# Two attention layers on one Trainium2 core: the second softmax by rows, its halves turned by DMA, outputs tile by tile

## The chip, the cores and the metric

The kernel runs on 1 core of one Trainium2 chip. The metric is the device time of one execution in microseconds (us). The engines are TensorE (PE, with its weight loads PEld), VectorE (DVE), ScalarE (ACT), GpSimd (POOL) and the sequencer that issues most DMAs, SyncE (SP).

## The reference

Input x has 8 images of 32 x 32 tokens and 256 channels. Two residual blocks follow one another; each begins with a group norm without weights.

```python
# block A: 32 windows (rows of the image), 8 heads of 32 channels
qkv = einsum('bnwc,cd->bnwd', gn(x), w_qkv)
attn = softmax(einsum('bhnqd,bhnkd->bhnqk', q, k) * 32 ** -0.5)
x = x + einsum('bnwc,cd->bnwd', attn_times_v, w_proj) + b_proj
# block B: all 1024 tokens, one head, q and k of 32 channels, v of 256
energy = einsum('bid,bjd->bij', k, q)
x = x + gamma * einsum('bij,bjc->bic', softmax(energy), v)
```

## The kernel before

One image after the other passes through both blocks, and three images are in work at once: in step `i` block B of image `i`, block A's attention of image `i+1` and the norm and q, k, v of image `i+2`. Each engine's program is written out by hand in this order: a function `first(i, ...)` and a function `second(i, ...)` per engine, called by `all_steps` (line 229), with a hardware loop over the steps 2 to 4. Engines run in order and meet in semaphores.

All products that need float32 accuracy are made of three f16 products, `split3` (lines 250 to 252): high by high, high by low, low by high. A tensor therefore exists as a high half and a low half (the rest).

**Block A** of an image: `transposes`, statistics and norm (`a_nh`, `a_nl`), q/k projection (`a_project_qk`, 48 products of 512 columns into `pa`), V projection (`a_project_v`, 48 of 256), `a_scores` (line 461, after `k_spread` has laid k out as a block diagonal by 8 DMAs), softmax in windows of 32 (`a_maximum`, `a_exponential`, `a_row_sum`, `a_probabilities` on POOL, `a_transpose`), `p_spread` (8 DMAs, line 340), `a_output` (line 484), the output's high parts on ACT (`a_out_high`, line 718) and low parts on DVE (`a_out_low`, line 875), `a_regroup` (16 DMAs, line 318), `a_projection` (48 products of 256 columns) and the residual (`a_residual`, line 884).

**Block B**: `transposes` of x1, norm, `b_project_qk`, `b_project_v`, `b_stacks` (4 DMAs, lines 304 to 307, which lay high and low of q and k above one another). Then the energies are made twice. `b_energy` (line 536) makes them by rows, only for the maximum of each row, `b_maximum` (line 904). The maxima are put as two more rows into `k_stack` (`b_max_rows`, line 543), and `b_energy_T` (line 554) makes the energies again, transposed and with the maximum taken off. ACT makes the exponential, which is then already in the layout that the output product needs: `e_h` (line 743) on ACT for five of the eight tiles and as a cast on DVE for three, `e32` (line 744), and the rest `e_l` on DVE (line 919). `b_output` multiplies all eight tiles of `e` with V; a 257th column of ones in V gives the row sum. `b_result` on DVE divides and adds.

In step `i` the `first` half of PE holds the outputs of image `i-1` with the energies of image `i` between them, the `second` half the transposed energies of image `i` with the projections of the other two images between them. So block B of one image stretches over two steps.

Of the kernel before, what the change touches and what calls it, by code (L numbers as in the profile page):

```python
# [35 lines left out]
P = 128  # L36
# [9 lines left out]
DVE_HIGH = (1, 3, 4)  # L46
VCOL = CH + 2
EPS = 1e-5
ROW_SCALE = 2.0 ** 15
# [6 lines left out]
def build(nc, x, w_qkv, w_proj, b_proj, wq1, wk1, wv1, gamma, ident_d, group_d, masks_d, out):  # L56
# [3 lines left out]
    with ExitStack() as ctx:  # L60
# [3 lines left out]
        def sem(name):  # L64
            return ctx.enter_context(nc.semaphore(name))

# [23 lines left out]
        xb = sb("xb", [P, TILES, CH])  # L90
        x1 = sb("x1", [P, TILES, CH])
# [17 lines left out]
        y = sb("y", [P, TILES, CH])  # L109
# [4 lines left out]
        q_stack = sb("q_stack", [P, TOKENS], F16)  # L114
        k_stack = sb("k_stack", [P, TOKENS], F16)
        v_h, v_l = sb("v_h", [P, TILES, VCOL], F16), sb("v_l", [P, TILES, VCOL], F16)
        max_neg = sb("max_neg", [P, TILES])
        max_hl = sb("max_hl", [P, TILES, 2], F16)
        ident_h = sb("ident_h", [P, P], F16)
        e32 = sb("e32", [P, 2, TOKENS])  # L120
        e_h, e_l = sb("e_h", [P, TILES, TOKENS], F16), sb("e_l", [P, TILES, TOKENS], F16)
        y_inv = sb("y_inv", [P, TILES])
        y_fac = sb("y_fac", [P, TILES])

# [5 lines left out]
        stage = e_l[:].rearrange("p t n -> p (t n)").bitcast(F32)  # L130
# [15 lines left out]
        s_ident = sem("s_ident")  # L146
# [10 lines left out]
        a_load = [sem(f"a_load{c}") for c in range(CHUNKS)]  # L157
        a_xb = sem("a_xb")
# [22 lines left out]
        b_copy = sem("b_copy")  # L181
# [9 lines left out]
        b_mxh = sem("b_mxh")  # L191
        b_mxl = sem("b_mxl")
        b_row = sem("b_row")
        b_rows = sem("b_rows")
        b_st = sem("b_st")
        b_exp = sem("b_exp")
        b_eh = sem("b_eh")
        b_el = sem("b_el")
        b_pv = sem("b_pv")
        b_yinv = sem("b_yinv")  # L200
        b_yfac = sem("b_yfac")
        b_y = sem("b_y")
# [20 lines left out]
        bufs = {"a": dict(src=xin, xT=a_xT, nh=a_nh, nl=a_nl, ps=pa, col=384, mean=3, var=2, **norm["a"], **{"s_" + k: v for k, v in n_["a"].items()}),  # L223
                "b": dict(src=x1, xT=b_xT, nh=b_nh, nl=b_nl, ps=pb, col=0, mean=2, var=3, **norm["b"], **{"s_" + k: v for k, v in n_["b"].items()})}

        def after(eng, s, value):

            if not (isinstance(value, int) and value <= 0):
                eng.wait_ge(s, value)

        def all_steps(eng, first, second):

            def peeled(half, i):
                half(i, *(0 <= n < IMAGES for n in (i, i - 1, i + 1, i + 2)))

            for i in range(-1, 2):
                peeled(first, i)
                peeled(second, i)
# [44 lines left out]
        def _(sp):  # L283
# [58 lines left out]
            def first(i, b, o, m, f):  # L342
                if m: p_spread(i + 1, 0)
# [782 lines left out]
```

## Time and profile before

| | us |
|---|---|
| median of 3 runs | 705.11 (704.42 to 709.46) |
| the profiled execution, its own time | 708.19 |
| its span, first to last instruction | 706.1 |
| PE busy in the span | 600.7 (85%) |
| DVE busy | 493.9 (70%) |
| ACT busy | 321.7 (46%) |
| POOL busy | 152.0 (22%) |

The rows come from the profiled execution; its own time is 2.1 us above its span. An engine's busy time counts its computing instructions alone. A PE product is shown longer than its share of the engine, since products are pipelined; the steps of the chain of work show the time between two of them. The granted clock is the share of TensorE's full clock. A DMA is issued by a sequencer (SPq is SP's), and "to landing" counts from the issue to the semaphore.

### The profile page before, as it was taken

To read this page: it belongs to the slowest core of one execution; us is meant where nothing else is said; L and a number is where in the kernel's file an instruction comes from. 1 tells how busy PE (TensorE), PEld (TensorE's weight loads), DVE (VectorE), ACT (ScalarE), POOL (GpSimd) and SP (SyncE) were. 2 spreads that over 40 slices of the span, in tenths; PEclk is the share of its full clock that TensorE was granted. 3 is DMA by queue.
4 is the path that set the end of the run, shared out by engine and by line. 5 is a ranking of instruction groups with operands and counts; after the bars stand their busy time and mean duration, and the time that the engine had idled before them with its cause. 6 is when DMAs were issued, how large, how long until landed. Compare 5 with 4: busy or idle time off the path is not lost. (4 is left out here: it accounts for less than half of the span.)

```text
span 706.1 us, 14862 instructions
## 1 busy us (share of the span) xinstructions
PE 600.7 (85%) x5859; PEld 433.6 (61%) x5859; DVE 493.9 (70%) x829; ACT 321.7 (46%) x422; POOL 152.0 (22%) x130
## 2 busy tenths in 40 slices
PE   2475794799998999899998999899989989649987
PEld 2255472547785677657774778567765767336756
DVE  4445267667976888577976797597967796775654
ACT  2423443476228741675228632774157611750261
POOL 5502232213114202303213311411230321000000
PEclk9996896789999999999999999999999999878999
DMA  4042313231241225031323223122504103201101
GB/s 156 0 121 61 90 32 94 50 82 38 84 105 51 61 54 145 33 88 31 104 82 82 51 82 104 48 56 48 145 26 105 31 24 106 76 0 38 43 4 60
DMA packets 40306, 47.51 MB, mean 67 GB/s; under 512 B 6848, under 2 KB 32320, under 8 KB 40256
## 3 DMA queue, kind: packets, MB, share of 16 engines
q1 hardware_dynamic: 36960, 43.47, 23.5%
q10 hardware_dynamic: 3296, 3.34, 1.4%
q8 instruction: 35, 0.57, 0.4%
q14 instruction: 15, 0.12, 0.1%
HBM read 10.09 MB, written 8.39 MB: 26 GB/s over the span
## 5 line engine op out<-in xcount | busy, mean ns | idle before, releaser
L250 PE MATMUL pb<-v_h,e_h 128*128 128x257 f16 x464 | 127.6, 275 | 1.7 <-DVE y L929 1.6
L252 PE MATMUL pb<-v_h,e_l 128*128 128x257 f16 x464 | 126.5, 273 | 0.0
L251 PE MATMUL pb<-v_l,e_h 128*128 128x257 f16 x464 | 126.1, 272 | 0.0
L904 DVE TENSOR_REDUCE max_neg<-pb 128x1 f32<-128x1024 f32 x64 | 77.5, 1210 | 42.6 <-PE pb L536 42.2
L919 DVE TENSOR_TENSOR e_l<-e,e_h 128x1024 f16<-128x1024 f32 x64 | 77.8, 1223 | 18.9 <-ACT e L744 17.3
L744 ACT ACTIVATE e<-pb,f_energy 128x1024 f32<-128x1024 f32 x64 | 71.3, 1114 | 23.1 <-PE pb L554 23.1
L554 PE MATMUL pb<-k_stack,q_stack 98*128 98x512 f16 x128 | 39.3, 389 | 29.8 <-ACT k_stack L735 19.9
L718 ACT ACTIVATE before_turn<-pa 128x1024 f16<-128x1024 f32 x16 | 15.5, 1021 | 106.5 <-PE pa L484 106.5
L1058 POOL TENSOR_TENSOR xb<-xin,bias 128x2048 f32<-128x2048 f32 x8 | 36.7, 4588 | 125.5 <-DVE x L884 125.5
L250 PE MATMUL pa<-a_nh,wqkv_h 128*128 128x512 f16 x128 | 52.1, 407 | 11.6 <-POOL a_nl L1051 11.6
L1063 POOL TENSOR_TENSOR before_turn<-before_turn,a_rinv 128x1024 f32<-128x1024 f32 x16 | 30.6, 1914 | 140.4 <-DVE a_rinv L865 140.4
L250 PEld LDWEIGHTS pb<-v_h,e_h 128*128 128x128 f16 x464 | 45.7, 99 | 18.0 <-issue 5.6
L536 PE MATMUL pb<-q_stack,k_stack 96*128 96x512 f16 x128 | 40.8, 402 | 18.6 <-DMA k_stack<-qk_hl 9.9
L743 ACT ACTIVATE e_h<-pb,f_energy 128x1024 f16<-128x1024 f32 x40 | 44.5, 1114 | 21.3 <-PE pb L554 21.2
L251 PEld LDWEIGHTS pb<-v_l,e_h 128*128 128x128 f16 x464 | 45.7, 98 | 10.5
L251 PE MATMUL pa<-a_nl,wqkv_h 128*128 128x512 f16 x128 | 51.5, 402 | 0.0
L252 PE MATMUL pa<-a_nh,wqkv_l 128*128 128x512 f16 x128 | 51.4, 402 | 0.0
L252 PEld LDWEIGHTS pb<-v_h,e_l 128*128 128x128 f16 x464 | 44.7, 96 | 6.9
L899 DVE TENSOR_TENSOR v_l<-pb,v_h 128x512 f16<-128x512 f32 x32 | 22.0, 687 | 37.8 <-ACT v_h L731 37.8
L1070 POOL COPY y<-x 128x512 f32<-128x512 f32 x32 | 24.7, 785 | 100.2 <-DMA out<-y 53.5
L1051 POOL TENSOR_TENSOR a_nl<-a_xT,a_nh 128x512 f16<-128x512 f32 x32 | 37.0, 1157 | 19.9 <-ACT a_xT L692 19.9
L484 PE MATMUL pa<-diag,v_tok 128*32 128x128 f32 x1024 | 34.7, 292 | 5.8 <-DMA diag<-turned 5.8
(135 smaller groups left out, 1365.6 us busy)
## 6 DMA issues: line engine op xcount, KB each, us to landing
xin<-in_x SPq DMA_DIRECT2D x16, 512.0 KB, 4.5
diag<-qkT SPq DMA_DIRECT2D x64, 128.0 KB, 2.3
diag<-turned SPq DMA_DIRECT2D x64, 128.0 KB, 2.4
turned<-before_turn SPq DMA_DIRECT2D x128, 64.0 KB, 2.0
out<-y SPq DMA_DIRECT2D x24, 256.0 KB, 2.1
out<-y ACTq DMA_DIRECT2D x8, 256.0 KB, 2.1
q_stack<-qk_hl SPq DMA_DIRECT2D x8, 128.0 KB, 2.3
k_stack<-qk_hl SPq DMA_DIRECT2D x8, 128.0 KB, 2.4
```

The costliest lines, as they stand in the source:

```text
L250: nc.tensor.matmul(out_ap, lh, rh, start=start, stop=False)
L251: nc.tensor.matmul(out_ap, lh, rl, start=False, stop=False)
L252: return nc.tensor.matmul(out_ap, ll, rh, start=False, stop=stop)
L484: last = nc.tensor.matmul(pa[32 * r:32 * r + 32, 2 * g + c, col:col + P].rearrange("p (w q) -> p w q", w=4), v_tok[:, t, h * DH:(h + 1) * ...
L536: last = nc.tensor.matmul(pb[:, c, :], k_stack[0:96, it * P:(it + 1) * P], q_stack[0:96, c * CHUNK:(c + 1) * CHUNK], start=True, stop=True)
L554: last = nc.tensor.matmul(pb[:, c, :], q_stack[0:98, jt * P:(jt + 1) * P], k_stack[0:98, c * CHUNK:(c + 1) * CHUNK], start=True, stop=True)
L743: nc.scalar.activation(e_h[:, jt, :], src, ACT.Exp, scale=f_energy[:, 0:1])
L744: nc.scalar.activation(e32[:, jt % 2, :], src, ACT.Exp, scale=f_energy[:, 0:1]).then_inc(b_exp, 1)
L904: nc.vector.tensor_reduce(max_neg[:, it:it + 1], pb[:, 0:2, :].rearrange("p a n -> p (a n)"), X, ALU.max, negate=True).then_inc(b_max, 1)
L919: nc.vector.tensor_tensor(e_l[:, jt, :], e32[:, jt % 2, :], e_h[:, jt, :], ALU.subtract).then_inc(b_el, 1)
L1051: nc.gpsimd.tensor_tensor(a_nl[:, ct, cols], a_xT[:, ct, cols], a_nh[:, ct, cols], ALU.subtract).then_inc(n_["a"]["nl"], 1)
L1058: nc.gpsimd.tensor_tensor(xb[:], xin[:], bias[:].unsqueeze(1).broadcast_to([P, TILES, CH]), ALU.add).then_inc(a_xb, 1)
```

## The change

Block B is done by rows with energies made once. `b_maximum` makes each row's negative maximum and, times `f_energy`, the bias of the exponential. ACT makes the exponential twice, as f16 (`row_h`, all eight tiles) and as f32 (`e32`). The low half `row_l` is made on DVE, for tiles 2 and 5 on POOL. Each half (128 rows of 1024) is turned by one DMA transpose into a slot of a ring of four, `e_t`. Then the output of this tile of rows can be made as soon as both halves are there. `row_h`, `row_l` and `e32` have two buffers each; `b_energy(k)` waits for the exponentials of tile `k-1`.

```diff
-            def b_max_rows(b):
-            def b_energy_T(b, jt):
...
-                    pe.wait_ge(b_max, nth(b, 8, it))
+                    pe.wait_ge(b_exp, nth(b, 8, k))
...
+            def turn_high(b, k):
+                sp.wait_ge(b_eh, nth(b, 8, k + 1))
+                sp.nop(nofuse=True)
+
+                after(sp, b_pv, nth(b, 8, k + 1 - SLOTS))
+                sp.nop(nofuse=True)
+                sp.dma_start_transpose(e_t[:, 0, k % SLOTS], row_h[:, k % 2, :]).then_inc(b_th[k % SLOTS], 16)
...
+            def b_exponential(b, k):
+                act.wait_ge(b_bias, nth(b, 8, k + 1))
+                bb, kk = tile_before(b, k, 2)
+                if bb >= 0:
+
+                    act.wait_ge(b_th[kk % SLOTS], turned_count(bb, kk))
+                    act.nop(nofuse=True)
+
+                    wait_row_low(act, bb, kk)
+                src = pb[:, 0:2, :].rearrange("p a n -> p (a n)")
+                nc.scalar.activation(row_h[:, k % 2, :], src, ACT.Exp, scale=f_energy[:, 0:1], bias=e_bias[:, k:k + 1]).then_inc(b_eh, 1)
+                nc.scalar.activation(e32[:, k % 2, :], src, ACT.Exp, scale=f_energy[:, 0:1], bias=e_bias[:, k:k + 1]).then_inc(b_exp, 1)
...
+            def b_output(b, k):
+
+                pe.wait_ge(b_th[k % SLOTS], turned_count(b, k))
+                pe.wait_ge(b_tl[k % SLOTS], turned_count(b, k))
...
+                for jt in range(TILES):
+                    last = split3(pb[:, 2 + k % 2, 0:CH + 1], (e_t[:, 0, s, jt, :], e_t[:, 1, s, jt, :]),
+                                  (v_h[:, jt, 0:CH + 1], v_l[:, jt, 0:CH + 1]), start=(jt == 0), stop=(jt == TILES - 1))
```

`turn_low` is `turn_high` for `row_l`, behind the low half's semaphore; `row_low(k)` waits until the low turn of tile `k-2` has landed. The result is copied from PSUM by ACT (`b_result_out`), DVE makes the factors for two tiles at once (`b_factors`), POOL multiplies and adds (`b_add`) into the buffer of x1, of which there are two (`x1_turns`); the copies into `y` are gone, all stores are issued by SP, and x is loaded a second time for the residual (`load_again`), where POOL adds the bias. V has two buffers as well. A's V projection goes to `pa` instead of `pb`.

The orders are written anew, as `stream(i, ...)` and `head(i, ...)`, and the hardware loop is gone: all steps are written out. PE's:

```python
            def stream(i, s, p, n, f):
                if s: b_energy(i, 0)
                if n: a_scores(i + 1)
                if p: b_output(i - 1, 5)
                if s: b_energy(i, 1)
                if p: b_output(i - 1, 6)
                if p: b_output(i - 1, 7)
                if s: b_energy(i, 2)
                if f: transposes("a", i + 2, range(4))
                if s: b_output(i, 0)
                if s: b_energy(i, 3)
                if s: b_output(i, 1)
                if n: a_output(i + 1, f, 0)
                if s: b_energy(i, 4)
                if s: b_output(i, 2)
                if f: group_mean("a", i + 2)
                if n: a_output(i + 1, f, 1)
                if s: b_energy(i, 5)
                if s: b_output(i, 3)
                if f: group_var("a", i + 2)
                if s: b_energy(i, 6)
                if s: b_output(i, 4)
                if s: b_energy(i, 7)
                if n: a_projection(i + 1)
```

`head` holds, on PE, in this order: x1's transposes with A's q/k projection of image `i+2` between and behind them, B's V projection (tiles 0, 1), B's q/k projection, B's V projection (2, 3), A's V projection of image `i+2`.

The queue of SP, around the sixteen regroup DMAs of one step in the middle. Before (`a_ol` counts the low parts of output A, `qk_hl` is what `b_stacks` sends):

```order
L277 DMA out<-y 128x2x256
L229 REGISTER_ALU [waits a_ol]
L318 DMA turned<-before_turn 32x2x512 [waits a_y]
L318 DMA turned<-before_turn 32x2x512 x15
L322 ISA
L330 DMA diag<-qkT 32x2x512 [waits a_ke,a_o]
```

With the change (`b_eh`, `b_el` and `b_elp` count the high halves and the low halves of DVE and of POOL):

```order
L357 DMA_TRANSPOSE e_t<-row_h 128x8x128 [waits b_eh,b_pv]
L327 DMA turned<-before_turn 32x2x512 [waits a_ol,a_y]
L327 DMA turned<-before_turn 32x2x512 x15
L365 DMA_TRANSPOSE e_t<-row_l 128x8x128 [waits b_elp,b_pv]
L357 DMA_TRANSPOSE e_t<-row_h 128x8x128 [waits b_eh,b_pv]
L365 DMA_TRANSPOSE e_t<-row_l 128x8x128 [waits b_el,b_pv]
L303 DMA out<-x_1 128x2x256 [waits b_y]
L357 DMA_TRANSPOSE e_t<-row_h 128x8x128 [waits b_eh,b_pv]
L365 DMA_TRANSPOSE e_t<-row_l 128x8x128 [waits b_el,b_pv]
```

The regroup now stands behind the high turn of tile 5, with five more turns behind it; eleven of a step's sixteen turns are ahead of it.

PE at the first product of A's projection, which waits for the regroup (`a_ox`), same step. Before:

```order
L252 MATMUL pa<-a_nh,wqkv_l 128x512
L554 MATMUL pb<-k_stack,q_stack 128x512 [waits b_exp]
L554 MATMUL pb<-k_stack,q_stack 128x512
L250 MATMUL pa<-wp_h,turned 128x256 [waits a_ke,a_ox]
L251 MATMUL pa<-wp_l,turned 128x256
```

With the change:

```order
L241 MATMUL pb<-v_h,e_t 128x257
L567 MATMUL pb<-q_stack,k_stack 128x512 [waits b_exp]
L567 MATMUL pb<-q_stack,k_stack 128x512
L239 MATMUL pa<-wp_h,turned 128x256 [waits a_ox]
L240 MATMUL pa<-wp_l,turned 128x256
```

Before, the projection stands between transposed energies, with q/k projections of the next image ahead; now it stands behind the last energies of the step and the output of tile 4, with all of A's q/k and V projections behind it.

DVE around the two low parts of output A (`before_turn<-pa,before_turn`). Before:

```order
L929 SCALAR_TENSOR_TENSOR y<-pb,y_fac,y 128x256 [waits b_yfac]
L875 TENSOR_TENSOR before_turn<-pa,before_turn 128x32x8x4 [waits a_oh]
L898 ISA
L899 TENSOR_TENSOR v_l<-pb,v_h 128x2x256 [waits b_vh]
L875 TENSOR_TENSOR before_turn<-pa,before_turn 128x32x8x4 [waits a_oh]
```

With the change:

```order
L275 TENSOR_TENSOR row_l<-e,row_h 128x1024 [waits b_exp,b_tl2]
L866 TENSOR_TENSOR before_turn<-pa,before_turn 128x32x8x4 [waits a_oh]
L818 TENSOR_SCALAR ave<-pb 128x2 [waits an_gv]
L894 TENSOR_REDUCE max_neg<-pb 128x1 [waits b_s]
L897 TENSOR_TENSOR e_bias<-max_neg,f_energy 128x1 [waits b_max]
L866 TENSOR_TENSOR before_turn<-pa,before_turn 128x32x8x4 [waits a_oh]
```

The second low part, which releases the regroup, stands behind the maximum of tile 6.

## Rows read from the trace of the kernel before

**Rows 1.** Windows: length, busy (x instructions) of PE, PEld, DVE, ACT, POOL, clock, DMA share, GB/s.

```profile
338.00:414.00 76.00, 70.81 (x734) 52.11 (x732) 59.63 (x102) 39.50 (x52) 17.80 (x15) 1.00 0.28 74
...
641.00:706.00 65.00, 57.24 (x462) 44.21 (x460) 36.73 (x74) 16.91 (x18) 2.88 (x4) 0.97 0.12 39
```

**Rows 2.** SP's queue in order of time: start us, us, what.

```profile
72.57 10.24 SPq L318 DMA_DIRECT2D turned<-before_turn  x16
...
337.89 0.52 SPq L304 DMA_DIRECT2D q_stack<-qk_hl  x1
...
349.98 2.43 SPq L340 DMA_DIRECT2D diag<-turned  x4
...
375.93 10.27 SPq L318 DMA_DIRECT2D turned<-before_turn  x16
...
413.94 0.52 SPq L304 DMA_DIRECT2D q_stack<-qk_hl  x1
```

**Rows 3.** PE in order of time: first energies of image 0, and a projection.

```profile
112.99 1.03 PE L536 MATMUL pb<-q_stack,k_stack 96*128 96x512 f16 x2 [5.82 <-DMA k_stack<-qk_hl]
...
388.29 0.27 PE L250 MATMUL pa<-wp_h,turned 128*128 128x256 f16 x1
```

**Rows 4.** The chain that ended last, in order of time: start us, us, what.

```profile
645.31 0.61 PE pb L536 x2
645.92 0.11 PE pb L250
...
677.66 0.21 PE pa L252
```

**Rows 5.** Groups by line and shape: xcount | busy us, mean ns | idle before, releasers.

```profile
L919 DVE TENSOR_TENSOR e_l<-e,e_h 128x1024 f16<-128x1024 f32 x64 | 77.8, 1223 | 18.9 <-ACT e L744 17.3
L904 DVE TENSOR_REDUCE max_neg<-pb 128x1 f32<-128x1024 f32 x64 | 77.5, 1210 | 42.6 <-PE pb L536 42.2
L744 ACT ACTIVATE e<-pb,f_energy 128x1024 f32<-128x1024 f32 x64 | 71.3, 1114 | 23.1 <-PE pb L554 23.1
...
L554 PE MATMUL pb<-k_stack,q_stack 98*128 98x512 f16 x128 | 39.3, 389 | 29.8 <-ACT k_stack L735 19.9 <-ACT e L744 9.5
L1051 POOL TENSOR_TENSOR a_nl<-a_xT,a_nh 128x512 f16<-128x512 f32 x32 | 37.0, 1157 | 19.9 <-ACT a_xT L692 19.9
...
L484 PE MATMUL pa<-diag,v_tok 128*32 128x128 f32 x1024 | 34.7, 292 | 5.8 <-DMA diag<-turned 5.8
...
L461 PE MATMUL pa<-diag,qkT 128*32 128x128 f32 x1024 | 29.6, 273 | 0.5 <-DMA diag<-qkT 0.5
...
L875 DVE TENSOR_TENSOR before_turn<-pa,before_turn 128x1024 f16<-128x1024 f32 x16 | 19.3, 1214 | 1.5 <-ACT before_turn L718 1.5
...
L677 ACT ACTIVATE b_xT<-pb 128x512 f32<-128x512 f32 x32 | 17.3, 598 | 12.8 <-PE pb L390 12.8
...
L390 PE MATMUL pb<-ident,x 128*128 128x128 f32 x128 | 17.0, 276 | 0.5 <-DVE x L884 0.5
...
L718 ACT ACTIVATE before_turn<-pa 128x1024 f16<-128x1024 f32 x16 | 15.5, 1021 | 106.5 <-PE pa L484 106.5
...
L543 PE MATMUL pb<-ident_h,max_hl 128*2 128x128 f16 x64 | 4.9, 219 | 0.4 <-DVE max_hl L911 0.4
```

**Rows 6.** DMA issues: what, count, KB each, median us from issue to landing.

```profile
turned<-before_turn SPq DMA_DIRECT2D x128, 64.0 KB, 2.0
...
q_stack<-qk_hl SPq DMA_DIRECT2D x8, 128.0 KB, 2.3
```

**Rows 7.** Windows of PE alone in the last step but one: busy, clock, DMA share, GB/s.

```profile
608.00:611.00 3.00, 0.60 (x2) 1.00 0.42 107
611.00:614.00 3.00, 1.36 (x4) 0.68 0.37 95
614.00:617.00 3.00, 2.60 (x13) 0.50 0.07 19
617.00:620.00 3.00, 3.00 (x18) 0.68 0.00 0
```

More of the change, by code:

```diff
@@ L45 @@
 GROUP = 8
-DVE_HIGH = (1, 3, 4)
+SLOTS = 4
+POOL_LOW = (2, 5)
+DVE_LOW = tuple(k for k in range(TILES) if k not in POOL_LOW)
 VCOL = CH + 2
 EPS = 1e-5
-ROW_SCALE = 2.0 ** 15
 def nth(b, per, n):
@@ L157, in build @@
         a_load = [sem(f"a_load{c}") for c in range(CHUNKS)]
+        a_again = [sem(f"a_again{c}") for c in range(CHUNKS)]
         a_xb = sem("a_xb")
@@ L222, in build, with all_steps @@
         )} for k in "ab"}
-        bufs = {"a": dict(src=xin, xT=a_xT, nh=a_nh, nl=a_nl, ps=pa, col=384, mean=3, var=2, **norm["a"], **{"s_" + k: v for k, v in n_["a"].items()}),
-                "b": dict(src=x1, xT=b_xT, nh=b_nh, nl=b_nl, ps=pb, col=0, mean=2, var=3, **norm["b"], **{"s_" + k: v for k, v in n_["b"].items()})}
+        bufs = {"a": dict(xT=a_xT, nh=a_nh, nl=a_nl, ps=pa, col=384, **norm["a"], **{"s_" + k: v for k, v in n_["a"].items()}),
+                "b": dict(xT=b_xT, nh=b_nh, nl=b_nl, ps=pb, col=0, **norm["b"], **{"s_" + k: v for k, v in n_["b"].items()})}
         def after(eng, s, value):
-            if not (isinstance(value, int) and value <= 0):
+            if value > 0:
                 eng.wait_ge(s, value)
[L231 to L238, printed above, removed]
-            with eng.Fori(2, IMAGES - 3) as i:
-                first(i, True, True, True, True)
-                second(i, True, True, True, True)
-            for i in range(IMAGES - 3, IMAGES + 1):
-                peeled(first, i)
-                peeled(second, i)
+        def all_steps(stream, head):
+            for i in range(-1, IMAGES + 1):
+                stream(i, *(0 <= k < IMAGES for k in (i, i - 1, i + 1, i + 2)))
+                head(i, *(0 <= k < IMAGES for k in (i + 1, i + 2)))
         def split3(out_ap, lhs, rhs, start=True, stop=True):
@@ L361, in _ @@
             load(0)
+            stream(-2, False, False, False, True)
             sp.wait_ge(s_pool, 6)
-            second(-2, False, False, False, True)
-            all_steps(sp, first, second)
+            head(-2, False, True)
+            all_steps(stream, head)
             for j in range(4):
@@ L1025, in _ @@
             weights_low((0,))
[L1026 removed]
+            stream(-2, False, False, False, True)
             weights_low(range(1, 5))
[L1028 to L1029 removed]
+            head(-2, False, True)
+            all_steps(stream, head)
         @block.gpsimd
```

692 lines of the change are left out of this document (317 added, 375 removed).

## The prediction

> **What bounds the kernel now.** I read the busy time by stretch first [rows 1]. A period from one image's stack DMA to the next is 76.05 us (337.89 to 413.94 [rows 2]); in it TensorE (PE) is busy 70.8 us of 76, VectorE (DVE) 59.6, ScalarE (ACT) 39.5, GpSimd (POOL) 17.8. So PE is the bound in the middle, with 5 us of holes. Before image 0's first energies lie 113.0 us [rows 3]; from image 7's first energies (645.3 [rows 4]) to the end are 60.8 us, and PE is busy 57 of the last 65 [rows 1].
>
> Next I asked which work covers the attention-A chain (scores, softmax, output, regroup, projection). In the SP queue [rows 2] the sixteen regroup DMAs start at 375.93 and take 10.27 us to issue; the projection that needs them starts at 388.3 [rows 3], 12.3 us after the start. In those 12.3 us PE does transposed energies, V and q/k projections: the wait is hidden.
>
> **The change, part by part.** PE prices at full clock: 0.11 us per 256- or 257-column product, 0.21 to 0.22 per 512-column one [rows 4].
>
> Removed on PE per image: sixteen transposed-energy products, 16 x 0.215 = 3.4 us, and the max rows, 4.9/8 = 0.6 us [rows 5]. PE work falls from 70.8 to 66.8 us.
>
> ACT: all eight high halves come from ACT (before 5 of 8), 3 x 1.11 = 3.3 us more, plus eight result copies of about 0.4 (257 columns, where 512 take 0.6): 39.5 + 6.5 = 46. DVE loses eight results (three small operations each), three casts and two of eight low halves (2.4), gains eight bias products of under 0.2 and four pairs of small ones: about 50. POOL gains two low halves (2 x 2.3, from 1.157 for 512 columns [rows 5]) and sixteen operations on 256 columns of about 0.55, loses the copies into `y`: about 28. None of these sums bounds an 80 us period; they matter where they stand in an order. The second load of x is two more DMAs per image beside a DMA share of 0.28 [rows 1]; on SP they stand ahead of turns that have 3 us to spare there, so I count nothing; without that cover it is 0.6 us each. The unrolled loop and the stores moved from ACT to SP I count at nothing too, for the same reason.
>
> What each tile now needs before the next tile's energies: energies 0.6, maximum 1.2, bias 0.2, two exponentials 2.2 [rows 5], so 4.4 us with handovers. Between E0 and E5 PE has more than that to do in each gap, so the chain costs nothing there; after E5 it is the path.
>
> A new stream, step by step from tile 0's energies (E0):
> 1. To E5 PE itself needs five energy pairs (2.2), scores 3.7 and output A 4.3 (29.6/8, 34.7/8), transposes 2.3, six output tiles of 24 x 0.11 = 2.64 (15.8): 28.3 us.
> 2. It also waits for turned halves. The low half of tile 2 stands in SP's queue behind eight `diag<-turned` DMAs, issued in 2.43 us per four [rows 2], themselves behind the DVE transposes (done about 18.6 by the order of DVE's work); the low half of tile 1 stands before them. A DMA transpose is in no row of before. Lower bound: one plain DMA, 0.5 to 0.6 us of issue and 2.3 to landing [rows 2, 6]. Nearest by bytes and by its cross-partition pattern: the regroup moves 1 MB in 16 DMAs of 64 KB, so a 256 KB half counts as four, 2.6 us of issue and about 4.0 to landing. Far bound: one issue per block of 128 columns, 8 x 0.64 = 5.1 and 6.8. A plain DMA starts that late that PE waits 2.8 us; 2.6/4.0 makes it 7.5. One instruction of 128 partitions resembles the first, a crossing of partitions the second: I take the middle, 5.0. E5 then starts at 33.3.
> 3. Output A's second half ends just before E5. ACT's high copies 2.0, two exponentials of tile 5 2.2, E6 0.6, maximum and bias 1.5, then the second low part on DVE 1.25 (the order puts it behind tile 6's maximum): 7.6. The regroup may start at 40.9.
> 4. The regroup then costs its 12.3 us to the projection. E7 has been issued by about 42, tile 4's output before it, and outputs 5 to 7 stand behind the next E0: PE has nothing to do for about 11 us. This is the main term: what was hidden is exposed. Behind it on SP wait the turns of tiles 5 to 7, whose outputs come after the next E0. But DVE's low half 7 waits until the turn of low half 5 has landed, and residuals 2 and 3 stand behind it: 40.9 + 10.3 + 3.1 = 54.3, while those residuals are due near 56: no cost, and 2 us if a turn takes 5.1/6.8.
> 5. From projection to next E0 PE does projection 5.3, transposes B 2.1, A's q/k 48 x 0.215 = 10.3, A's V 5.3, B's V 5.3, B's q/k 2.6: 31 us, and about 1.5 of holes (projection tiles 2 and 3 wait for residuals, the group mean for its statistics). The norm chain and the stacks (4 DMAs, 4.4 us) end about 2 us before A's V, so they cost nothing.
> 6. The clock. In the step before the last one [rows 7], PE is busy 0.60 of 3 us from 608 and 1.36 of 3 from 611; the granted clock goes from 1.00 to 0.50 (1.2 instead of 2.4 GHz) near 613 and is back near 618. Five us at half speed lose 2.5. Each period now has such a hole: 2.5.
>
> Period: 40.9 + 12.3 + 32.5 + 2.5 = 88.2 us; with the cheap turn 86, with the four-DMA turn 91.
>
> Ends. Image 0: its regroup ends as before (72.57 + 12.3 = 84.9 [rows 2]), but image 1's q/k projection now follows it instead of covering it: first energies at 84.9 + 32.5 + 2 = 119.5 instead of 113. The last interval lacks A's work for a next image (15.6 on PE) and becomes a chain: 88.2 - 7 = 81. Tail from E0 of image 7: eight tiles of 4.4 to 4.5 and the rest of the last, 37.5; low half 1.3, turn 3.1, output 2.7, copy and factors 0.9, GpSimd for two tiles 2.5, store 2.6: 51 instead of 60.8. Sum: 119.5 + 6 x 88.2 + 81 + 51 = 780.7 of span against 706.1, with the 2.1 us around it 783 against that execution's 708.2. The median of the runs is 3 us lower (705.11), so I say 780.
>
> Two statements of the Trainium skill pull at step 2. "Advanced Engine Details and Errata", section X-Bar Transpose (TRN2), says transposing DMAs run about as fast as ordinary ones, at 350 to 400 GB/s: an estimate for 256 KB is 0.7 us of moving, which is the lower bound, period 86. "VectorE: DVE Perf Modes", The three transpose paths, gives 1309 ns for one 128x128 block of two-byte values: if eight follow one another, an estimate of 10.5 us a half, beyond my far bound, and some 1400 us for the kernel. No row of before can decide.
>
> **The rivals.**
> R1, turns bind SP. Each half is handled block by block, 5.1 us of issue. SP then spends 16 x 5.1 = 82 us plus 44 plain DMAs of 0.6 (26): 108. The regroup stands behind eleven turns, 3.3 + 56 + 9 = 68 after E0; with 12.3 and 35 the period is 115, the time about 119.5 + 6 x 115 + 110 + 90 = 1010. For it: SP's queue has an issue time of 0.6 even for small DMAs. Against: one instruction does a whole half. Chance 0.13.
> R2, the other side: TensorE stays the bound, since the hole of step 4 is filled or does not arise. That takes outputs ready early and output A before tile 4, so that the regroup starts below about 30 after E0. Then a period is 76.05 less 4.0, 72, the tail 10 less, the start 3 more: 706 - 28 - 10 + 3 = 671. It decides from a period of about 77.5 down (breaking even: start 6.5 more, tail 10 less). For it: PE was the bound and loses 4 us. Against: in after's order nothing of PE stands between E7 and the projection. Chance 0.10.
> R3, half of that: softmax A runs ahead of my hand order and the regroup starts near 30 to 32, with a period of 77 to 78: within 1%. Chance 0.05.
> My forecast, a period of 82 to 96: 0.72.
>
> **How the numbers follow.** A measurement of this kernel tells about 1% from no change. Slower is forecast plus R1: 0.85; faster 0.10; same 0.05. The forecast's own range is 740 to 845. To hold 8 in 10 I go down toward R3 and R2 to 725, and up toward R1 to 885; what lies in R2 and in the dear part of R1 is left out, some 0.2.
>
> **What would show it.** Right: about 11 us of PE idle per image ended by DMA `turned<-before_turn`, PE clock 0.5 for a few us behind it; SP's regroup starting about 41 after E0; a period near 88; no transposed energies; the first energies near 119. Wrong in a size: the turn's issue and landing differ from 1.3 and 3.1; the wait before outputs 1 and 2 tells it. Wrong in kind: turns queued on SP with PE or ACT waiting for `e_t` in every tile (R1), or PE busy over 90% of the period (R2).

## The result and the profile after

| | us |
|---|---|
| changed kernel, median of 4 runs | 820.21 (815.71 to 822.36) |
| kernel before, median of 4 runs beside it | 704.91 (704.42 to 709.46) |
| ratio | 1.16, 95% interval 1.156 to 1.164 |
| predicted | 780 (725 to 885) |

The changed kernel is 115 us slower. The direction, the kind and the main term were as predicted, the size 5% too small.

The page of the changed kernel (span 819.0 us): busy time of each engine, DMA packets and the chain that ended last.

```profile
PE 599.4 (73%) x5667; PEld 442.4 (54%) x5667; DVE 457.6 (56%) x708; ACT 374.9 (46%) x502; POOL 280.9 (34%) x250
...
DMA packets 183940, 89.70 MB, mean 110 GB/s; under 512 B 142272, under 2 KB 175936, under 8 KB 183872
...
PE 48%; SPq 13%; DVE 11%; POOL 10%; ACT 6%; DMA 6%; issue 5%; POOLq 0%; ACTq 0%; DVEq 0%
```

PE is busy as long as before (600.7 us), but in a span 113 us longer: less work at a lower clock, and holes. SP's queue and POOL now stand in the chain.

The windows of one middle step, image 5's energies to image 6's, which answer to [rows 1] and [rows 7] (length, busy, clock, DMA share, GB/s):

```profile
488.00:580.00 92.00, 72.83 (x706) 54.38 (x705) 56.69 (x86) 46.17 (x62) 34.65 (x30) 0.89 0.54 120
...
488.00:506.00 18.00, 17.44 (x248) 1.00 0.39 90
506.00:524.00 18.00, 12.26 (x123) 0.81 0.80 161
524.00:533.00 9.00, 5.97 (x97) 1.00 0.78 205
533.00:551.00 18.00, 8.95 (x45) 0.62 0.58 124
551.00:580.00 29.00, 28.20 (x201) 1.00 0.37 83
```

The step takes 92 us where it took 76; PE idles 19 us of them instead of 5. PE is full in the first and last stretch alone. The lines behind the first are windows of PE alone. Two stretches have a mean clock between 0.50 (1.2 GHz) and 1.00 (2.4 GHz), since a part of each ran at either level, and in each PE had waited before.

SP's queue in the same step, which answers to [rows 2]:

```profile
509.50 0.38 SPq L303 DMA_DIRECT2D out<-x  x1
510.03 1.30 SPq L357 DMA_TRANSPOSE e_t<-row_h  x1
511.49 4.99 SPq L349 DMA_DIRECT2D diag<-turned  x8
516.63 1.30 SPq L365 DMA_TRANSPOSE e_t<-row_l  x1
...
535.47 10.72 SPq L327 DMA_DIRECT2D turned<-before_turn  x16
```

The stacks of this step started at 482.10 and the next ones at 574.53, so the regroup starts 53.4 us after the stacks and the next stacks 39.1 after the regroup: 92.4. (All eight stacks: 112.50, 202.42, 294.38, 388.78, 482.10, 574.53, 665.94, 756.36; the mean interval is 92.0.) An issue of a turn takes 1.3 us.

The same two ways in the kernel before, and what PE does in them (first the kernel before, then the changed one):

```profile
337.89:375.93 38.04, 33.55 (x377) 26.50 (x375) 29.62 (x57) 13.14 (x19) 11.07 (x11) 1.00 0.31 86
375.93:413.94 38.01, 37.31 (x360) 25.65 (x359) 30.06 (x46) 26.36 (x34) 6.73 (x4) 1.00 0.25 62
```

```profile
482.10:535.47 53.37, 41.79 (x518) 34.01 (x517) 36.66 (x51) 26.82 (x35) 26.10 (x20) 0.92 0.61 136
535.47:574.53 39.06, 31.46 (x194) 20.75 (x193) 20.02 (x36) 19.54 (x30) 8.55 (x10) 0.85 0.43 96
```

The way back from the regroup is as long as before: on the mean of six steps 39.3 us beside 39.2. All of the longer step lies ahead of the regroup, 53.0 beside 37.5. There PE is busy 8 us longer and waits more; behind the regroup, where its work used to be the cover (37.3 busy of 38.0), it is busy 6 us less.

PE in the same step, which answers to [rows 3]: energies of tiles 0, 4, 5 and 7, and the projection.

```profile
488.26 0.60 PE L567 MATMUL pb<-q_stack,k_stack 96*128 96x512 f16 x2
...
519.25 0.76 PE L567 MATMUL pb<-q_stack,k_stack 96*128 96x512 f16 x2
...
525.99 0.61 PE L567 MATMUL pb<-q_stack,k_stack 96*128 96x512 f16 x2
...
540.23 0.60 PE L567 MATMUL pb<-q_stack,k_stack 96*128 96x512 f16 x2
547.62 0.40 PE L239 MATMUL pa<-wp_h,turned 128*128 128x256 f16 x1 [6.80 <-DMA turned<-before_turn]
```

The groups that answer to [rows 5], with the idle time before them and what ended it:

```profile
L239 PE MATMUL pb<-v_h,e_t 128*128 128x257 f16 x512 | 154.9, 303 | 56.4 <-issue 56.3
L1030 POOL TENSOR_SCALAR y_raw<-y_raw,y_fac 128x256 f32<-128x256 f32 x64 | 73.7, 1152 | 278.6 <-DVE y_fac L904 278.6
...
L239 PE MATMUL pa<-wp_h,turned 128*128 128x256 f16 x128 | 42.5, 332 | 64.6 <-DMA turned<-before_turn 64.6
...
L523 PE MATMUL pa<-diag,v_tok 128*32 128x128 f32 x1024 | 39.1, 316 | 21.0 <-DMA diag<-turned 21.0
...
L1032 POOL TENSOR_TENSOR x<-y_raw,x 128x256 f32<-128x256 f32 x64 | 49.3, 771 | 5.3
```

PE is idle for 220 us of the span, before for 105. Three waits are new or longer: for the regroup (64.6 us, 15.9 of them once and some 7 in each other image), ahead of the output tiles, where the instruction waits for turned halves (56.3, shown as "issue"), and for the spread of the scores (21.0, before 5.8). The DMA issues, median from issue to landing, beside [rows 6]:

```profile
e_t<-row_h SPq DMA_TRANSPOSE x64, 3.2
```

The low halves land in 3.2 us as well.

### The profile page after: what moved, and what is told of

Its sections match the earlier page's. It is cut to its first block, busy times and chain, and to the rows that moved or that the text cites. A ratio compares the mean times of both kernels' runs of the same rounds, so it can differ in the third digit from the quotient of the medians.

```text
span 819.0 us, 14569 instructions
## 1 busy us (share of the span) xinstructions
PE 599.4 (73%) x5667; PEld 442.4 (54%) x5667; DVE 457.6 (56%) x708; ACT 374.9 (46%) x502; POOL 280.9 (34%) x250
## 2 busy tenths in 40 slices
DMA packets 183940, 89.70 MB, mean 110 GB/s; under 512 B 142272, under 2 KB 175936, under 8 KB 183872
## 3 DMA queue, kind: packets, MB, share of 16 engines
q10 hardware_dynamic: 1120, 1.25, 0.5%
## 4 chain that ended last, share of the span: by engine, by line
PE 48%; SPq 13%; DVE 11%; POOL 10%; ACT 6%; DMA 6%; issue 5%; POOLq 0%; ACTq 0%; DVEq 0%
SPq L327 9%; PE pa L239 7%; PE pa L240 7%; PE pa L241 7%; PE pb L239 5%; PE pb L240 5%; PE pb L241 5%; PE pa L523 5%; POOL y_raw L1030 5%; PE pa L500 3%; POOL before_turn L1025 3%; DMA diag<-turned 2%; DVE max_neg L894 2%; POOL x L1032 2%; DMA turned<-before_turn 2%
## 5 line engine op out<-in xcount | busy, mean ns | idle before, releaser
L239 PE MATMUL pb<-v_h,e_t 128*128 128x257 f16 x512 | 154.9, 303 | 56.4 <-issue 56.3
L1030 POOL TENSOR_SCALAR y_raw<-y_raw,y_fac 128x256 f32<-128x256 f32 x64 | 73.7, 1152 | 278.6 <-DVE y_fac L904 278.6
L240 PE MATMUL pb<-v_l,e_t 128*128 128x257 f16 x512 | 154.0, 301 | 0.0
L241 PE MATMUL pb<-v_h,e_t 128*128 128x257 f16 x512 | 153.6, 300 | 0.0
L717 ACT ACTIVATE row_h<-pb,e_bias,f_energy 128x1024 f16<-128x1024 f32 x64 | 77.0, 1204 | 155.3 <-DVE e_bias L897 154.5
L239 PEld LDWEIGHTS pb<-v_h,e_t 128*128 128x128 f16 x512 | 54.6, 107 | 84.0 <-issue 71.5
L239 PE MATMUL pa<-wp_h,turned 128*128 128x256 f16 x128 | 42.5, 332 | 64.6 <-DMA turned<-before_turn 64.6
L718 ACT ACTIVATE e<-pb,e_bias,f_energy 128x1024 f32<-128x1024 f32 x64 | 76.5, 1196 | 0.0
L240 PEld LDWEIGHTS pb<-v_l,e_t 128*128 128x128 f16 x512 | 55.0, 107 | 12.5 <-issue 0.3
L241 PEld LDWEIGHTS pb<-v_h,e_t 128*128 128x128 f16 x512 | 54.7, 107 | 12.6
L275 DVE TENSOR_TENSOR row_l<-e,row_h 128x1024 f16<-128x1024 f32 x48 | 58.5, 1219 | 1.4 <-ACT e L718 1.4
L523 PE MATMUL pa<-diag,v_tok 128*32 128x128 f32 x1024 | 39.1, 316 | 21.0 <-DMA diag<-turned 21.0
L1032 POOL TENSOR_TENSOR x<-y_raw,x 128x256 f32<-128x256 f32 x64 | 49.3, 771 | 5.3
L1014 POOL TENSOR_TENSOR a_nl<-a_xT,a_nh 128x512 f16<-128x512 f32 x32 | 36.7, 1154 | 36.6 <-ACT a_xT L666 36.6
```

Source lines behind the costliest of these rows:

```text
L239: nc.tensor.matmul(out_ap, lh, rh, start=start, stop=False)
L240: nc.tensor.matmul(out_ap, lh, rl, start=False, stop=False)
L241: return nc.tensor.matmul(out_ap, ll, rh, start=False, stop=stop)
L275: eng.tensor_tensor(row_l[:, k % 2, :], e32[:, k % 2, :], row_h[:, k % 2, :], ALU.subtract).then_inc(done, 1)
L523: last = nc.tensor.matmul(pa[32 * r:32 * r + 32, 2 * g + c, col:col + P].rearrange("p (w q) -> p w q", w=4), v_tok[:, t, h * DH:(h + 1) * ...
L717: nc.scalar.activation(row_h[:, k % 2, :], src, ACT.Exp, scale=f_energy[:, 0:1], bias=e_bias[:, k:k + 1]).then_inc(b_eh, 1)
```

## The experiments

All are edits of the changed kernel, but for e7. Steps are told by two numbers from SP's queue: from the stacks (L313) to the regroup's start, and from there to the next stacks. They are those of one middle step of each trace; from step to step of one trace each varies by 1 to 3 us, so where the reading of a difference needs it, the mean of six steps stands beside it.

| kernel | median, us | ratio, 95% interval | stacks to regroup + regroup to stacks |
|---|---|---|---|
| changed | 820.21 | 1.16 [1.156, 1.164] | 53.4 + 39.1 |
| e1_straight | 756.15 | 1.0698 [1.0623, 1.0773] | 53.4 + 31.8 |
| e2_plain | 810.46 | 1.1473 [1.1401, 1.1545] | 52.1 + 40.1 |
| e3_bias | 817.77 | 1.1574 [1.1497, 1.1652] | 52.5 + 39.5 |
| e6_fill | 818.43 | 1.1572 [1.1483, 1.166] | 55.1 + 38.4 |
| e5_store | 816.73 | 1.1588 [1.1544, 1.1632] | 53.4 + 39.3 |
| e4_split | 771.93 | 1.0877 [1.0842, 1.0911] | 53.4 + 32.9 |
| e8_order | 768.82 | 1.0884 [1.083, 1.0937] | 41.9 + 43.1 |
| e9_both | 752.43 | 1.0664 [1.0629, 1.0699] | 41.8 + 40.6 |
| e12_parts | 752.72 | 1.0631 [1.0586, 1.0677] | 43.1 + 41.6 |
| e10_head | 764.12 | 1.0777 [1.0753, 1.0802] | 49.9 + 36.6 |
| e11_head_sp | 805.05 | 1.1353 [1.1301, 1.1405] | 49.6 + 41.7 |

### e1: the regroup's price

```diff
-                    for s in range(4):
-                        sp.dma_start(o_dst[32 * s:32 * s + 32, r], o_src[32 * r:32 * r + 32, :, s]).then_inc(a_ox, 16)
+                    sp.dma_start(o_dst[:, r], o_src[:, :, r]).then_inc(a_ox, 16)
```

> The regroup is four DMAs of 256 KB, each copying 128 partitions straight (the same bytes, without the crossing of partitions, so block A's projection gets other data), instead of sixteen of 64 KB. Theory (the exposed regroup, issue time first): its issue falls from 10.3 us to about 2.5, the projection starts 6.8 to 7.5 us earlier in each of 8 steps, so 760 to 766 us. Rival (the projection would be held near the same time by tile 7's energies or something else of the step): 800 us or more.

Measured: 756.15 us, 64 less than the changed kernel and 4 better than the theory's range. SP's queue and PE of e1:

```profile
496.76 2.80 SPq L326 DMA_DIRECT2D turned<-before_turn  x4
```

```profile
501.62 0.60 PE L566 MATMUL pb<-q_stack,k_stack 96*128 96x512 f16 x2
502.06 0.27 PE L239 MATMUL pa<-wp_h,turned 128*128 128x256 f16 x1
```

The way to the regroup is unchanged to a tenth; all the gain lies behind it: it takes 2.80 us to issue instead of 10.7, and the projection starts 5.3 us after it instead of 12.2. The projection no longer waits for the regroup here: it follows the energies of tile 7 at once, and in the whole run PE waits 10.2 us for the regroup, 8.8 of them in one place. The exposed regroup is the largest single cost, 64 of the 115 us. With it out of the way the kernel is still 51 us slower than the one before.

### e7: the same edit in the kernel before

```diff
-                    for s in range(4):
-                        sp.dma_start(o_dst[32 * s:32 * s + 32, r], o_src[32 * r:32 * r + 32, :, s]).then_inc(a_ox, 16)
+                    sp.dma_start(o_dst[:, r], o_src[:, :, r]).then_inc(a_ox, 16)
```

> The control of e1: the kernel before, with its regroup of sixteen 64 KB transfers in place of four straight 256 KB ones (the axes are not regrouped, so the projection reads other values; the amount moved is the same). Theory: in the kernel before the regroup lies beside TensorE's transposed energies, V and q/k projections, so shortening it by 8 us an image gives nothing: 698 to 706 us. Rival: the regroup is as much on the path there as in the changed kernel, and e1's 64 us were not caused by its being exposed: 640 to 680 us.

Measured: 708.27 us against 705.76, ratio 1.0028 [1.0005, 1.0052]: no gain, and 2 us above the theory's range. In SP's queue of e7 the regroup is as short as in e1, and the stacks (338.90 and 414.94) are 76.0 us apart, as before:

```profile
376.93 2.76 SPq L317 DMA_DIRECT2D turned<-before_turn  x4
```

So the same transfers cost nothing in the one order and 64 us in the other. With e1 this shows the main term: what was hidden is exposed.

### e2: the turns as plain transfers

```diff
-                sp.dma_start_transpose(e_t[:, 0, k % SLOTS], row_h[:, k % 2, :]).then_inc(b_th[k % SLOTS], 16)
+                sp.dma_start(e_t[:, 0, k % SLOTS].rearrange("p t n -> p (t n)"), row_h[:, k % 2, :]).then_inc(b_th[k % SLOTS], 16)
```

and the same for the low half.

> Each DMA transpose is replaced by a plain DMA of the same 256 KB (the output product gets unturned data). Theory (a turn costs SP 1.25 us and lands after 3.2, so it is cheap): a plain one costs 0.6 and 2.3, which takes 1 to 2 us from each period at the outputs that wait for e_t: 803 to 812 us. Rival (the turns are what slows the kernel): 760 us or less.

Measured: 810.46 us, 10 less, as the theory said. The transfers now land in

```profile
e_t<-row_h SPq DMA_DIRECT2D x64, 256.0 KB, 2.4
```

(the low halves in 2.3) and not in 3.2 us. Turning costs little over moving: R1 is refuted in kind, and the turn's size in the prediction held.

### e3: the bias as a one-tensor operation

```diff
-                nc.vector.tensor_tensor(e_bias[:, k:k + 1], max_neg[:, k:k + 1], f_energy[:, 0:1], ALU.mult).then_inc(b_bias, 1)
+                nc.vector.tensor_scalar(e_bias[:, k:k + 1], max_neg[:, k:k + 1], f_energy[:, 0:1], None, ALU.mult).then_inc(b_bias, 1)
```

> The bias product on DVE is made by tensor_scalar (one tensor operand and a per-partition scalar) instead of tensor_tensor. In the trace the 128x1 product takes 0.16 us as a rule, but 1.8 us when GpSimd runs a two-tensor operation beside it, until that one ends; in a middle step this happens twice on the way to the regroup. Theory (it waits for the port that GpSimd holds, as an operation with two SBUF tensors): 1.6 to 3.3 us less per period, 795 to 807 us. Rival (the stretching is of the trace, or any DVE operation has it): 817 to 822 us.

What led to it, in DVE's and POOL's timeline of the changed kernel:

```profile
527.89 0.16 DVE L897 TENSOR_TENSOR e_bias<-max_neg,f_energy 128x1 f32<-128x1 f32 x1
...
532.42 1.78 DVE L897 TENSOR_TENSOR e_bias<-max_neg,f_energy 128x1 f32<-128x1 f32 x1
534.12 1.21 DVE L866 TENSOR_TENSOR before_turn<-pa,before_turn 128x1024 f16<-128x1024 f32 x1
```

```profile
532.07 2.12 POOL L275 TENSOR_TENSOR row_l<-e,row_h 128x1024 f16<-128x1024 f32 x1
```

The one-column product takes 0.16 us at the least, and 1.78 where it starts beside POOL's low half, and ends with that. Behind it stands the cast that releases the regroup. In e3 all 64 take the same time:

```profile
L897 DVE TENSOR_SCALAR e_bias<-max_neg,f_energy x64: 212/214/215, 121.2 to 797.2; 128x1 f32<-128x1 f32 x64
```

The stretched product is gone, and the time is 817.77 us, in the rival's range, though not for the rival's reason, and within the spread of the changed kernel: the regroup starts 0.9 us earlier in the step, and 0.4 of them are lost behind it (1.0 and 0.3 on the mean of six steps). The stretched product was real, but most of its 1.6 us did not lie on the path: in the changed kernel SP's turn ahead of the regroup ends at 534.51, only 1.0 us ahead of its start.

### e6: a filler for the hole

Two groups of A's q/k projection (2.6 us of PE) go ahead of A's projection.

```diff
+                if f: a_project_qk(i + 2, 0, (0, 1))
                 if n: a_projection(i + 1)
...
-                if f: a_project_qk(i + 2, 0, (0,))
...
-                if f: a_project_qk(i + 2, 0, (1,))
```

> Two of A's q/k projection groups of the next-but-one image (2.6 us of PE) stand ahead of A's projection, in the hole, instead of behind it. Theory of the prediction (PE bounds the way from the projection to the next energies): 2.6 us less in each of six periods, 804 us. Rival (that way is bound as much by the norm chain and the stacks, as the last interval hints, which has no such PE work and is still 90 us): 815 to 820 us.

Measured: 818.43 us, the rival's. PE work taken out of the way from the projection to the next energies gives back 0.7 us of 2.6 in this step (38.4 for 39.1) and nothing on the mean of six steps (39.6 for 39.3). PE of e6 at the group mean of x1's norm, behind the projection and the transposes:

```profile
554.63 0.38 PE L438 MATMUL pb<-bmv,group_avg 128*128 128x2 f32 x2 [2.38 <-DVE bmv L800]
```

In the changed kernel PE waits 0.8 us there, here 2.38, and the projection runs at the lower clock at first in both. So that way is not bound by PE alone, as my step 5 had it: DVE's statistics are ready 10.8 us behind the projection's first product, in the changed kernel 11.5. The whole run is 1.8 us below the changed kernel's median, inside the spread of both.

### e5: one store moved

```diff
-                if p: store_pair(i - 1, 3)
                 if n: p_spread(i + 1, 0)
                 if n: p_spread(i + 1, 1)
+                if p: store_pair(i - 1, 3)
```

> The changed kernel, with one SP instruction moved: the store of output pair 3 goes behind the spread of the score groups to p_all. Theory: the store waits for GpSimd's last residual and holds the spread, which is ready about 3 us earlier; the spread feeds output A, output A the regroup, so each image gains 1 to 3 us: 800 to 812 us. Rival: output A waits for something else as well (TensorE's own order up to it), and the time stays at 815 to 822.

Measured: 816.73 us, the rival's. PE of e5, energies of tiles 0, 4 and 5:

```profile
484.20 0.60 PE L567 MATMUL pb<-q_stack,k_stack 96*128 96x512 f16 x2
...
511.97 0.60 PE L567 MATMUL pb<-q_stack,k_stack 96*128 96x512 f16 x2
515.52 0.27 PE L239 MATMUL pb<-v_h,e_t 128*128 128x257 f16 x1 [2.94 <-issue]
...
521.92 0.60 PE L567 MATMUL pb<-q_stack,k_stack 96*128 96x512 f16 x2
```

E4 comes 27.8 us after E0 instead of 31.0: the wait for the spread is gone. E5 comes 37.7 us after E0, exactly as without the edit. Output 2 now waits 2.9 us (1.2 before) for the low half of tile 2, whose turn stands behind the spread's eight transfers, so it starts only 1.7 us earlier, 31.3 after E0 instead of 33.0. Those 1.7 go to the clock: from output 2 to E5 it is 6.4 us instead of 4.75, at a granted clock of 0.76 from 515 to 522. Another wait and the lower clock took the place of the first wait.

### e4: half of the regroup from ScalarE's queue

```diff
-                for r in range(4):
+                for r in range(2):
                     for s in range(4):
                         sp.dma_start(...)
...
                 if s: b_exponential(i, 6)
+                if n: a_regroup_rest(i + 1)
```

`a_regroup_rest` has the same waits as `a_regroup` and issues the other eight.

> The changed kernel in its own order, with half of the regroup's sixteen transfers issued from ScalarE's queue (behind the exponential of tile 6) instead of SP's. Theory: the exposed 12 us of the regroup are mostly issue, 0.64 us a transfer on one queue, so two queues take up to 5 us off each of eight images: 780 to 790 us. Rival (from e9, where the same split gained only 2 us an image): ScalarE is held for 6 us by its own issues, the exponential behind them comes late, or the transfers are slower side by side; 800 to 815 us.

Measured: 771.93 us, 48 less and better than the theory. The regroup as SP's and ScalarE's queues issue it, and the projection behind it:

```profile
508.81 5.45 SPq L327 DMA_DIRECT2D turned<-before_turn  x8
```

```profile
508.81 5.15 ACTq L739 DMA_DIRECT2D turned<-before_turn  x8
```

```profile
515.71 0.28 PE L239 MATMUL pa<-wp_h,turned 128*128 128x256 f16 x1 [1.33 <-DMA turned<-before_turn]
```

From the regroup's start to the projection 6.9 us instead of 12.2. The first step gains as well (its stacks start at 107.68, in the changed kernel at 112.50). Behind the shorter hole the projection runs at full clock from its first product on (0.28 us, 0.40 in the changed kernel), and the granted clock of the step from 455 to 542 is 0.94, where the changed kernel has 0.89. On the mean of six steps the way back from the regroup is 33.7 us beside 39.3.

### e8 and e9: another order

e8, beside e5's edit, moves calls in four engines. PE: both halves of `a_output` directly behind energies 4 (in the changed kernel one stands ahead of them, the other behind output 2), and output 4 behind the projection. DVE: both `a_out_low` ahead of `group_mean`. SP: the regroup ahead of `turn_low(4)`, `turn_high(5)` and the store of pair 0. ACT: `a_out_high` ahead of result 2, result 4 behind the norm. e9 adds e3's edit and e4's split, here behind exponential 5.

```diff
                 if s: b_energy(i, 4)
+                if n: a_output(i + 1, f, 0)
+                if n: a_output(i + 1, f, 1)
                 if s: b_output(i, 2)
...
                 if n: a_projection(i + 1)
+                if s: b_output(i, 4)
```

> The changed kernel with the same work in another order, which gives attention A's chain priority: output A ahead of output tile 2, its casts ahead of result 2, the regroup ahead of the turn of high half 4 and the stores, output tile 4 behind the projection, so that TensorE has something to do while the regroup runs. Theory (the time lies in the chain from the first energies to the regroup's start, 47 us, and in the bare regroup of 12): 7 to 10 us less per image, 745 to 770 us. Rival (the order doesn't matter, since the tile chain energies, maximum, bias, exponential sets the pace): 800 to 820.

> e8's order, with half of the regroup's transfers issued from ScalarE's queue (behind the exponential of tile 5) and the bias product as a one-tensor operation. Theory: the regroup's time is mostly the issue of sixteen transfers on one queue (10 of 12 us), so two queues at once take 5 us off each image beyond e8: 705 to 735 us. Rival: the transfers themselves are the limit, or ScalarE loses as much in its exponentials as SP gains: like e8, 745 to 770.

Measured: e8 768.82 us, as its theory said; e9 752.43, 16 less, short of its theory and in its rival's range. In e8 the regroup starts 11.5 us earlier in the step, but only 7.4 of them arrive, since the way behind it is 4.0 longer. Output 4 (2.65 us, from 517.14 in e8) now stands between the projection and the transposes of x1, the first 20 products of the projection run at the lower clock instead of 13 (0.7 us), and from the regroup's start to the projection it is 12.7 us instead of 12.2. In e9 ScalarE's issues hold it: its exponential of tile 6 starts behind its last issue, energies 7 wait for that, and the projection stands directly behind them.

```profile
484.12 4.75 ACTq L739 DMA_DIRECT2D turned<-before_turn  x6
488.99 0.38 ACT L729 ACTIVATE y_raw<-pb 128x257 f32<-128x257 f32 x1 [4.16 <-issue]
```

```profile
491.62 1.03 PE L567 MATMUL pb<-q_stack,k_stack 96*128 96x512 f16 x2 [6.13 <-ACT e L718]
```

### e12: ScalarE's issues and the projection out of each other's way

```diff
+                if n: a_regroup_rest(i + 1)
                 if s: b_exponential(i, 5)
-                if n: a_regroup_rest(i + 1)
...
+                if n: a_projection(i + 1, (0, 1))
                 if s: b_energy(i, 7)
-                if n: a_projection(i + 1)
+                if n: a_projection(i + 1, (2, 3))
```

and A's first two residuals ahead of the last maximum.

> e9's kernel with ScalarE's eight regroup transfers ahead of the exponential of tile 5 instead of behind it, and A's projection ahead of the last energies in its first half, behind them in its second. Theory (in e9 ScalarE's issues start at 482.7 and end at 488.9 while SP's ended at 487.2; the exponential of tile 6 stands behind them, so the last energies come at 491.6 and the projection, in order behind them, at 492.4): the regroup lands 2 to 4 us earlier and no longer meets the tile chain, 725 to 740 us. Rival: the exponential of tile 5 is then 3 us late and everything behind it in the tile chain too, so that the sum stays: 748 to 760 us. In neither case is it faster than the kernel before.

Measured: 752.72 us, the rival's. In the middle step ScalarE's eight issues took 6.15 us (5.15 in e4); over the run the transfers land in 4.0 us (median) instead of 2.0, SP's in 3.9, and exponential 5 waits 6 us behind the issues:

```profile
turned<-before_turn ACTq DMA_DIRECT2D x64, 64.0 KB, 4.0
```

```profile
491.38 1.21 ACT L718 ACTIVATE row_h<-pb,e_bias,f_energy 128x1024 f16<-128x1024 f32 x1 [6.02 <-issue]
```

### e10 and e11: the way from the projection to the scores

B's q/k projections alternate with its V, the stacks go ahead of half of the key spread, and the first two energies ahead of A's scores, with most of A's V projection between them.

```diff
                 if s: b_energy(i, 0)
+                if n: a_project_v(i + 1, (1, 2, 3))
+                if s: b_energy(i, 1)
                 if n: a_scores(i + 1)
```

> e9's kernel with a new order between projection and scores: B's q/k projections alternate with the first two groups of its V, its stacks go ahead of the second half of A's key spread, the first energies go behind one quarter of A's V projection and the second ones behind the rest, ahead of A's scores; output tile 4 goes ahead of A's projection, and the low turn of tile 4 ahead of the regroup. Theory: the way back from the projection to the first energies (33 us in e9) is shorter by 3 to 5 us, and VectorE is less crowded in A's softmax; 4 to 6 us less per image than e9, 705 to 725 us. Rival: what is gained ahead of the scores is lost behind them, since A's loop (scores, softmax, output, regroup, projection) sets the period and only the tile chain starts earlier: 740 to 755 us.

> e10 with the whole regroup on SP's queue again. Theory: the split over two queues is worth the 2 us an image that e9 had over e8: e10 plus 10 to 25 us. Rival: ScalarE's 6 us of issue ahead of exponential 6 cost as much as they save, now that TensorE has tile 4's output to do in the hole: within 5 us of e10.

Measured: 764.12 and 805.05 us. e10 is slower than e9, past its own rival: on the mean of six steps the way behind the regroup is 4.6 us shorter (35.7 for 40.3), but the one to it 6.6 longer (49.3 for 42.7). That fits the rival's reason, that A's loop from the scores to the projection and back sets the step and what is put ahead of the scores holds it up; no run separates it from the other moves of e10. e11 beside e10 is 41 us slower, more than both its theory (10 to 25) and its rival (5) allowed: here the split over two queues is worth nearly what it was in e4.

No version beats the kernel before. The best, e9 and e12, are 6 to 7% slower.

## Why the prediction was right, and where its sizes were off

By its own terms, in the middle step shown above and in us:

| term | predicted | measured |
|---|---|---|
| first energies of image 0 | 119.5 | 118.7 |
| E0 to E5 | 33.3 | 37.7 |
| E5 to the regroup's start | 7.6 | 9.5 |
| regroup to projection | 12.3 | 12.2 |
| projection to next E0, with the clock's 2.5 | 35.0 | 33.1 |
| step | 88.2 | 92.4 |
| last interval, E0 of image 6 to E0 of image 7 | 81 | 88.2 |
| tail from E0 of image 7 | 51 | 58.7 |

On the mean of its six steps, from E0 to E0, the step is 92.2 us. The span is 38.3 us longer than the 780.7 of the sum: 24 in the six steps, 7.2 in the last interval, 7.7 in the tail, less 0.8 at the start. Within the step 6.3 us too little ahead of the regroup stand against 1.9 too much behind it, so a part of the nearness of 88.2 is luck.

**Right.** The main term, step 4: the regroup's 12.3 us, hidden before, are exposed. e1 takes 64 us out with it, the same edit in the kernel before (e7) nothing, the split of e4 48. The size of a turn, step 2: 1.3 and 3.1 us were taken, 1.3 and 3.2 measured, and e2 shows that it matters little, so R1 is out. ("VectorE: DVE Perf Modes" of the Trainium skill, section The three transpose paths, gives 1309 ns for a 128x128 block: eight blocks do not follow one another here, since the half lands after 3.2 us. "Advanced Engine Details and Errata", section X-Bar Transpose (TRN2), has such transfers about as fast as others: by that rule, the trace agrees within 0.8 us, 3.2 beside 2.4.) The turns show in the packets, 183940 where e2 has 67205 and the kernel before 40306; the DMA share of a step is 0.54, in e2, which moves the same bytes unturned, 0.40, before 0.28. R2 and R3 fell as predicted: PE has 19 us of holes.

**The clock, step 6, was looked for in one place and counted too high there.** I had read one drop a step out of [rows 7]; there are two, at a mean granted clock of 0.81 from 506 to 524 and of 0.62 from 533 to 551. In busy time they cost more than my 2.5 us: the step has 72.8 us of busy PE where the work of step 1 is 66.8 at full clock, 6.0 more (weighed by the two windows, 12.26 x 0.19 + 8.95 x 0.38 = 5.7). But most of the slow products stand ahead of a wait that ends no earlier if they are faster. PE in the middle step, output A's first half and output 2, then the projection's second product:

```profile
515.90 3.42 PE L523 MATMUL pa<-diag,v_tok 128*32 128x128 f32 x64 [1.95 <-DMA diag<-turned]
...
521.24 0.27 PE L239 MATMUL pb<-v_h,e_t 128*128 128x257 f16 x1 [1.23 <-issue]
...
547.81 0.42 PE L240 MATMUL pa<-wp_l,turned 128*128 128x256 f16 x1
```

Output 1 is slow ahead of the wait for the spread, the first half of output A (3.42 us, the second half at full clock 1.95) ahead of the wait for low half 2, and output 4 ahead of the 6.80 us for the regroup. Only the first 13 products of the projection, 0.21 us apart instead of 0.11, stand on the way: some 1.4 us, where I had 2.5. So the 4.2 us a step that I missed are not the clock's. The hole is in two parts: 6.8 us at the projection, and 4.1 at output 4, which waits for a low half whose turn stood on SP behind the first store, held by POOL.

**The waits ahead of E5, step 2, had the right cause and too short a time.** Low half 2 behind the spread was named, and it sets E5 here: output 2 starts 33.0 us after E0, and from there PE works without a pause to E5, 4.75 us. What came later than I had it is the spread, issued from 511.49, 23.2 us after E0. DVE's transposes were done at 20.3, where I took 18.6, and SP stood until 509.5 at a store that waits for POOL, with high turn 2 behind it. The turn of low half 2 was issued at 516.63, and PE could go on 4.6 us later; the median landing is 3.2, but here the DMA share is 0.96 (515 to 524). PE's wait of 1.95 us for the spread itself, ahead of E4, I had not named. e5 takes the store out of its way, and low half 2 and the lower clock keep E5 where it was.

**Step 3 was short by 1.9 us**, of which the bias product held by POOL is 1.6; e3 removed it and won 0.9. Of the sums of busy time per step ACT's came out (46.2 us beside 46); DVE has 56.7 where I had about 50, and POOL 34.7 where I had about 28. Neither bounds the step, but POOL's operations hold stores, and with them SP's queue.

**The last interval and step 5.** I said a chain, 7 us less once A's work for a next image is gone. Instead the last interval is 88.2 us from E0 to E0, and 90.4 from stacks to stacks, 39.3 of them behind the regroup as in the other steps. Lines of the chain in that interval, start and length in us:

```profile
729.43 0.21 PE pa L241
...
743.15 0.73 POOL br L1001
...
748.76 0.21 PE pb L239
```

With A's products gone, 28 products of the projection and 21 of B's V are made at 1.2 GHz (0.21 us a product, 0.11 at full clock [rows 4]; granted clock 0.71 from 729 to 745), which costs some 5 us. Between them the norm passes through DVE, ACT and POOL, and PE waits for it three times, 7.3 us in all, where it waits 0.8 in the middle step. The clock and these waits together took what A's q/k projection had freed behind the regroup (10.3 us), and e6 shows in a middle step as well that PE's work there is not the only bound.

**The tail, 7.7 us**, and POOL. I had priced its 256-column operations at 0.55 us; the rows above say 1.15 and 0.77. At the end of the kernel two tiles take 3.3 us on it instead of 2.5. The clock is 0.90 from 755 to the end, of 41.3 us busy: some 4 more, as an estimate. The rest is not settled.

**Open.** In e1, where PE hardly waits for the regroup, 51 of the 115 us are left, with steps of 84.5 us on the mean beside 76.7 before. How they divide among the waits for turned halves, the wait for the spread and the lower clock was not separated. e9 missed its theory by 17 us; ScalarE's held exponentials and the slower transfers (3.0 and 3.3 us to landing, 2.0 in the changed kernel) stand in its trace, but the share of each was not tried.

## What to carry to other kernels

A transfer that costs nothing has a cover by name: write down which work covers it, and where an edit takes that work away, count the transfer in full. Issue time on one queue is latency when the chain is bare (0.64 us each here), and a second queue is worth most where the engine whose queue it is has nothing due that others wait for: 48 us in e4, 16 in e9 together with e3's edit. When one wait is taken out and the time stays, look a few instructions on for the one that took its place. Where holes are predicted, look for the lower clock behind each of them, and count it only where the slow products stand on the way to what everything waits for.

## What the runs showed of the hardware

- A DMA transpose of 128 rows of 1024 f16 values between two tiles in SBUF: a median of 1.25 to 1.3 us of issue and 3.2 us to landing (3.0 to 4.9); the plain transfer of the same 256 KB took 0.5 to issue and lands in 2.4 (e2).
- A DVE product of two one-column tensors took 0.16 us at the least and up to 1.81; the one of 1.78 shown above ran beside a two-tensor operation on POOL and ended with it. With a scalar operand in place of the second tensor it took 0.21 at all 64 places (e3).
- POOL's scaling of 256 columns took 0.92 us at the least and up to 1.96.
- Sixteen transfers of 64 KB took 10.3 to 11.0 us to issue on one queue, and eight on each of two 5.2 to 5.5, in one step up to 6.8 (e4). In e12, with the same eight and eight, it was 5.2 to 7.5, and the median landing 4.0 us instead of 2.0.
- The same slow products cost nothing or all of their time: of some 6 us of busy time that the lower clock added to a middle step, about 1.4 stood on the way to the next energies.
